# The two transfers of the softmax shift: both begun by SyncE, or the second by ScalarE

## The reference

```python
# layer 1: attention in a window of 128 keys
scores = jnp.einsum('bhtd,bhsd->bhts', q, k) * scale
allowed = (j <= i) & (j >= i - WINDOW)
attn = jax.nn.softmax(jnp.where(allowed[None, None], scores, -jnp.inf), axis=-1)
x = _layernorm(x + (attn @ v) @ w_out.T)
# layer 2: causal attention, then the two best of 8 experts for each token
x_resid = x + causal_attention(_layer_norm(x, ln1_g, ln1_b)) @ w_o
xf = _layer_norm(x_resid, ln2_g, ln2_b)
out = sum(gate_e[:, None] * (gelu(xf @ w1[e] + b1[e]) @ w2[e] + b2[e]) for e in range(8))
x = _layernorm(x + out + x_resid)
```

## Time and profile before

| | us |
|---|---|
| median of 3 runs | 778.16 |
| lowest, highest | 774.82, 779.01 |
| the profiled execution | 781.22 |
| its span in the trace | 779.4 |

### The profile page before, as it was taken

How to read it: one execution, slowest core, us unless ns; L and a number is a source line. 1 busy time by engine, 2 the same in 40 slices (tenths; PEclk the granted TensorE clock), 3 DMA queues, 4 the chain that set the end, 5 groups by cost and what they waited for, 6 DMA issues and landing times.

```text
span 779.4 us, 20482 instructions
## 1 busy us (share of the span) xinstructions
PE 636.2 (82%) x7679; PEld 389.1 (50%) x7679; DVE 569.5 (73%) x1318; ACT 463.8 (59%) x773; POOL 424.0 (54%) x646
## 2 busy tenths in 40 slices
PE   2578998999988788989888988988687997899760
PEld 1333544544444343444444443444247997899750
DVE  2664787887887989898889798988544775555573
ACT  3044776767776566766666667667773563455433
POOL 5035566666765534245555464656854655444662
PEclk8577999999999999999999899999998998999995
DMA  6744744664362553424334352510211223222745
GB/s 201 183 127 80 191 135 92 160 172 127 76 176 66 116 141 79 140 59 139 83 119 105 99 125 95 130 50 12 62 49 45 56 70 87 58 70 61 146 73 161
DMA packets 57549, 82.22 MB, mean 105 GB/s; under 512 B 7672, under 2 KB 48096, under 8 KB 54380
## 3 DMA queue, kind: packets, MB, share of 16 engines
q1 hardware_dynamic: 51228, 68.78, 34.8%
q0 software_dynamic: 5184, 11.61, 6.0%
q10 hardware_dynamic: 1040, 0.52, 0.2%
HBM read 43.55 MB, written 37.17 MB: 104 GB/s over the span
## 4 chain that ended last, share of the span: by engine, by line
PE 47%; DVE 18%; issue 11%; ACT 8%; DMA 8%; POOL 4%; SPq 2%; another core or an unknown queue 1%; POOLq 0%; DVEq 0%; ACTq 0%
PE side_ps L1475 9%; PE pair_ps L1624 8%; PE pair_ps L1636 8%; ACT probs L753 5%; PE pair_ps L1395 4%; DVE row_max L929 4%; PE pair_ps L1496 4%; DMA arena<-parts_dram 3%; DVE row_max L931 2%; DMA arena<-shift_t 2%; PE pair_ps L1455 2%; PE pair_ps L1420 2%; DVE row_max L934 2%; PE side_ps L1535 2%; POOL rows_dram L657 2%
## 5 line engine op out<-in xcount | busy, mean ns | idle before, releaser
L753 ACT ACTIVATE probs<-pair_ps 128x1024 f32<-128x1024 f32 x272 | 275.9, 1022 | 126.6 <-PE pair_ps L1395 122.8
L1475 PE MATMUL side_ps<-probs,v_aug 128*32 128x256 f32 (+3 forms) x2048 | 163.7, 415 | 9.2 <-POOL probs L645 4.0
L880 ACT ACTIVATE arena<-pair_ps,arena 128x128 f32<-128x128 f32 x284 | 81.0, 369 | 85.9 <-PE pair_ps L1624 62.4
L1395 PE MATMUL pair_ps<-arena 50*128 50x256 bf16 (+3 forms) x1024 | 107.9, 287 | 21.2 <-DMA arena<-shift_t 7.2
L632 POOL TENSOR_SCALAR_AFFINE_SELECT probs<-probs 128x512 f32<-128x512 f32 x96 | 61.4, 640 | 112.6 <-ACT probs L753 111.7
L698 POOL DMA_INDIRECT outputs_dram<-arena x71 | 70.8, 997 | 75.8 <-DVE arena L1276 56.7
L920 DVE TENSOR_REDUCE row_max<-pair_ps 128x4 f32<-128x768 f32 x96 | 89.0, 950 | 28.5 <-PE pair_ps L1429 28.0
L1624 PE MATMUL pair_ps<-arena 128*128 128x128 f32 x568 | 80.7, 288 | 19.2 <-issue 8.2
L1624 PEld LDWEIGHTS pair_ps<-arena 128*128 128x128 f32 x568 | 73.3, 202 | 22.1 <-issue 18.7
L929 DVE TENSOR_REDUCE row_max<-pair_ps 128x2 f32<-128x1024 f32 x64 | 76.6, 1219 | 10.0 <-PE pair_ps L1455 7.0
L1395 PEld LDWEIGHTS pair_ps<-arena 50*128 50x128 bf16 x1024 | 32.5, 95 | 100.3 <-issue 42.2
(11 more groups left out here) (178 smaller groups left out, 1043.0 us busy)
## 6 DMA issues: line engine op xcount, KB each, us to landing
arena<-parts_dram SPq DMA_DIRECT2D x96, 192.0 KB
parts_dram<-parts SPq DMA_DIRECT2D x32, 384.0 KB
parts_dram<-parts SPq DMA_DIRECT2D x32, 256.0 KB
pack<-in_pack SPq DMA_DIRECT2D x8, 578.0 KB, 10.2
arena<-rows_dram SPq DMA_DIRECT2D x71, 65.0 KB
parts_dram<-parts SPq DMA_DIRECT2D x32, 128.0 KB
arena<-parts_dram SPq DMA_DIRECT2D x32, 128.0 KB
resid<-outputs_dram POOLq DMA_DIRECT2D x6, 512.0 KB
```

Of the source, the lines that this page charges most:

```text
L753: nc.scalar.activation(probs[:, n % PROBS, :], pair_ps[RING_AT["score", n][0]][:, :, :].rearrange("p b t -> p (b t)"), ACT.Exp, scale=SCAL ...
L880: last = nc.scalar.activation(hidden[n % H_DEPTH][:, f * BLK:(f + 1) * BLK], hidden_ps[n % 2][:, f * BLK:(f + 1) * BLK], ACT.Gelu_apprx_ta ...
L1395: last = nc.tensor.matmul(pair[:, r, col:col + width], k_st[u % STACKS][own, gs, j * P:(j + 1) * P], q_st[u % STACKS][own, gs, q0:q0 + wid ...
L1475: last = nc.tensor.matmul(o_ps[c * VHEAD:(c + 1) * VHEAD, q0:q0 + width], v_aug[u % 2][:, j, first:first + VHEAD], probs[:, slot, r * T + ...
```

## The change

```diff
             def load_shift(u):
                 sp.wait_ge(misc_taken, JOB["shift", u])
-                for r in range(TILES_R):
-                    sp.dma_start(q_st[u % STACKS][HALF * r + STACK_K:HALF * r + SCORE_K, :, :],
-                                 shift_t[2 * GS * r:2 * GS * (r + 1), :]).then_inc(shift_in[u % STACKS], 16)
+                sp.dma_start(q_st[u % STACKS][STACK_K:SCORE_K, :, :], shift_t[0:2 * GS, :]).then_inc(shift_in[u % STACKS], 16)
...
                 nc.scalar.activation(shift_t[:, :], misc[0:4 * GS, :], ACT.Copy).then_inc(misc_taken, 1)
+                act.wait_ge(misc_taken, JOB["shift", u])
+                act.dma_start(q_st[u % STACKS][HALF + STACK_K:HALF + SCORE_K, :, :], shift_t[2 * GS:4 * GS, :]
+                              ).then_inc(shift_in[u % STACKS], 16)
```

## The result

The changed kernel takes **785.18 us** (median; 780.19 to 790.47), beside 777.58 us (771.21 to 781.42) for the kernel before on the same chip. The ratio is 1.0107, with a 95% interval of 1.0083 to 1.0130: slower by 1.1%, 6 to 10 us, 7.6 us by the medians. The profiled execution took 785.21 us (span 783.5), 4.0 us more than that of before, which itself lay 3.1 us above its median.

A forecast was written before the change was run, and what follows sets the result against it. TensorE was about half of the chain, waiting repeatedly on ScalarE through three score buffers, and 7.2 us for shift rows. Gains 0.81 minus losses 5.16 made 4.35 us slower: 778.16 + 4.35 = 782.5 us, range 778.3 to 788.

The forecast's parts named there:

- the short issue: Rival: ScalarE's issue takes only 0.42 us; +1.6 us, 779.8; chance 0.27 together with the wait off the path.
- engines of their own for the second transfer: Rival: second transfer lands 0.67 us earlier, with a short copy wait and issue; -2.1 us, 776.1; chance 0.05.
- issues that take turns: Rival: the two issues need something in common, nothing lands earlier, exponential 1.5 us late; +13 us, 791.5; chance 0.10.
- the wait off the path: Rival: at copies 9 to 12 VectorE could run ahead; +2.6 us, 780.8; chance 0.27 together with the short issue.
- D, the exponential's lateness: Behind ScalarE's copy of each unit's shift: the exponential starts 0.87 us later, bounds 0.59 to 1.5; issue 0.70.
- The landing: End of the shift's second transfer: two bursts sharing two DMA engines end 0.21 us earlier; ends 0 and 0.67.
- Copies 3 to 6: ScalarE's shift copies of units 3 to 6: later maxima use up most of TensorE's row wait; gain 0.42 us together.
- Copy 7: ScalarE's shift copy of unit 7: rows not waited for, late exponential delays maxima that VectorE takes; loss 0.70 us.
- Copies 0, 2 and 8: ScalarE's shift copies of units 0, 2, 8: TensorE waits less for the rows; gains 0.21, 0.16 and 0.02 us.
- Copies 9 to 12: Shift copies of units 9 to 12: late exponential delays the maxima; losses 2.61 us for 9 to 11, 0.81 at 12.
- Copies 13 and 14: Shift copies of units 13, 14: same wait, but the ranking product already waits 0.44 for VectorE; loss 2 x 0.43 us.
- Copy 15: Shift copy of unit 15: ScalarE is busy without a gap, so the last unit's first exponential starts later; loss 0.18 us.

The follow-up runs named there:

- the filled kernel: Changed kernel plus 20 unread matmuls in TensorE's causal wait for the late exponential; 775.11 us, 1.0003, and a second time 776.25 us, 1.0012, against the kernel before.
- local copies alone: Against the changed kernel, ScalarE issues the second transfer for units 0 to 8 only, SyncE the rest; 777.38 us, 0.9979; second run 775.67 us, 1.0021.
- the first one to DRAM: Against the changed kernel, SyncE issues both transfers and ScalarE one extra of the same source and size to a DRAM scratch tensor; 781.17 us, 1.0042.
- causal copies alone: Against the changed kernel, ScalarE issues the second transfer only for copies 9 to 15, SyncE the rest; 789.37 us, 1.0149.

## Why the prediction was right, and where it was too small

The forecast was 782.5 us, 4.35 more than before, in a range of 778.3 to 788.0. Measured were 785.18, 7.6 to 8.3 more: the sign and the range held, the size was little more than half. The sign held by the mechanism that was forecast, a late exponential that the causal maxima wait for; that the range held is partly luck, since the lower clock, which makes up a good part of the loss, was not among the terms that set its upper end. The rivals fall: the short issue (0.62 measured, not 0.42), engines of their own for the second transfer (bursts back to back), issues that take turns (0.62 on both engines at once), and the wait off the path (the dose comes through whole).

- **D, the exponential's lateness:** 0.87 forecast, 0.85 to 0.88 measured. The parts were off and cancelled: the issue is 0.62 and not 0.70, since the factor of 1.08 from the output's transfer does not carry over, and 0.10 us instead of 0.05 lies behind it.
- **The landing:** 0.21 forecast; the bursts end 0.28 us earlier, and the copy-to-scores time is 3.39 us, 3.36 forecast.
- **Copies 3 to 6:** forecast 0.09 to 0.11 each. From the tables of copy times the intervals that began at copies 3 to 6 went from 26.58, 26.59, 26.57 and 29.06 to 28.58, 26.41, 26.45 and 28.84 us; the first is lengthened by a drop of the clock (0.88) that came and went between executions. So about 0.12 to 0.22 each where nothing disturbs.
- **Copy 7:** -0.70 forecast, and wrong. The step that failed is "VectorE, which takes them at 238.03": the reductions of the earlier trace rows read the maxima ahead of those that the late exponential releases. In the trace of after VectorE begins 0.59 us ahead of those maxima and goes on without a pause:

```profile
236.16 1.22 DVE L930 TENSOR_REDUCE row_max<-pair_ps 128x2 f32<-128x1024 f32 x1
237.35 0.96 DVE L932 TENSOR_REDUCE row_max<-pair_ps 128x2 f32<-128x768 f32 x1
```

```profile
236.75 0.34 PE L1450 MATMUL pair_ps<-first_b,eye_b 64*128 64x256 bf16 x4 [0.93 <-ACT probs L751]
```

  The first scores of unit 7 come 4.17 us behind copy 7, where it was 4.53. In sum the local copies gain about 1 us (0.17, 0.18, 0.12 and 0.22 from copies 3 to 6, the first of them against the filled kernel's 26.41, and 0.1 to 0.7 between copies 7 and 8, where the profiles with a clock of 0.95 have 35.96 to 36.11 us without the local issues and 35.40 to 35.83 with them, and once 33.93) instead of 0.1: an estimate from the profiles, too small for the times to confirm.
- **Copies 0, 2 and 8:** 0.21, 0.16 and 0.02 forecast, not readable in single profiles. The interval from copy 8 to copy 9 grew by 1.33 us, at a clock of 0.91 (0.96 before); with the same local issues it took 36.9 us at full clock in five other profiles.
- **Copies 9 to 12:** 0.87 each (0.81 at 12) forecast. At copy 9 it was 0.87. At 10 to 12 the two profiles differ by 0.34 to 0.59 only, but against the clean stretches (39.56, 38.94 and 39.40 us for these intervals in the second run with local copies alone) the changed kernel's 40.92, 41.05 and 41.42 are 1.36, 2.11 and 2.02 more.
- **Copies 13 and 14:** 0.43 each forecast, right at full clock (0.40 and 0.35), 2.00 and 1.91 in the change. **This is the term that was mis-sized**, and with it 10 to 12: the sum priced a wait by its own length and let what comes behind run as before. Behind a wait of 1.5 us the products run at the lower clock; they used up the slack of 0.44 and added to the loss.
- **Copy 15:** -0.18 forecast. TensorE waits there 1.60 us for the rows, as the only place, and the end behind copy 15 took 234.8 us beside 235.2. Nothing stands out of the scatter of that part (232 to 239 us over the profiles).

The trace of before held the warning. The slack of 0.44 stood in front of the ranking product after copy 13, while after copy 10 that product followed without a pause; in the clean profile of local copies alone it waits 0.44 after copy 10 as well. The same code, at the same wait of 0.65 us, has two different outcomes, and the difference was the granted clock in the windows. Read in time, it would have said that this part of the kernel stands at the edge of losing its clock, and that a base at copies 10 to 12 which had already lost it understates what a longer wait costs.

## What to carry to other kernels

An instruction put in front of one that another engine waits for costs its own time only as long as what follows keeps its speed: read the granted clock behind every wait of TensorE that a change will lengthen, in more than one place, look for another wait close ahead of it (the likely difference between copy 9 and the others here), and ask what the products behind it cost at the lower clock. Before putting a transfer's issue on a compute engine "since it has time", look for the instruction behind it; one place later it was free here. A wait that can't be shortened can be filled with matmuls that nobody reads: the changed kernel was about 9 us faster with them (5.8 us of it in the stretch where they stand), and the kernel before gained nothing.

## What the runs showed that was not expected

- Behind copies 10 to 14 TensorE's granted clock fell behind unfilled waits of 1.52 to 1.62 us at 17 of 17 places where it was still full; at copy 9 it stayed full behind 2.05 us. Where it is low, the next 5 us have 0.50 to 0.66 of full clock, and an interval grows by 1.4 to 2.1 us for a delay of 0.85.
- The first issue on ScalarE took 1.45 us in the changed kernel (1.45 to 1.47 in all eight profiles where ScalarE begins with this transfer at copy 0) and 1.52 with causal copies alone, against 0.62 for the following ones. Not every first one does: the output's in before took 0.42, and the first one to DRAM 0.34.
- The same 16 KB cost ScalarE 0.62 us to issue into 2 partitions of SBUF and 0.31 into a DRAM tensor of the same shape. On SyncE and ScalarE the same transfer costs the same.
